# Graph attention in fp32: squares of 2 KB per partition, loads and stores two tiles at a time, six of a slot's sixteen squares on ScalarE's queue

## The chip, the cores and the metric

The kernel runs on one core of a Trainium2 chip. The metric is the device time of one execution in microseconds, lower is better. Six units matter: TensorE (PE) multiplies matrices into PSUM; VectorE (DVE), ScalarE (ACT) and GpSimd (POOL) compute on the memory; SyncE (SP) only waits, counts and issues DMAs. DMAs are issued here from two queues, SP's and ACT's, and moved by 16 DMA engines. Each unit executes its own instructions in order and waits for others by semaphores.

## The reference

For 8 graphs of 1024 nodes with 384 features, six heads of width 64:

```
q, k, v = x @ Wq + bq, x @ Wk + bk, x @ Wv + bv
scores  = q @ k^T / 8 ; masked where adj is false
probs   = softmax(scores) ; ctx = probs @ v (per head)
out     = layernorm(x + ctx @ Wf + bf)
```

`adj` is a boolean matrix of 1024 x 1024 for each graph. All is in fp32.

## The kernel before

One batch is one graph. It is worked through in 24 slots. A slot `s` stands for one tile of 128 queries and one pair of heads: `s // 6` is the group of two query tiles, `s % 6 // 2` the pair of heads, `s % 2` the query tile. Batch 0 and batch 7 are written out, batches 1 to 6 are a loop on every engine. In all there are 8 x 24 = 192 slots.

In each slot:
- PE computes the scores of two heads into PSUM (`scores`, L479), in three products of a high and a low part each. They fill the only score buffer, so the next slot's scores wait until DVE has read them.
- DVE adds the mask and takes the row's minimum while it writes SBUF (`mask_scores`, L671), once for each head.
- ACT takes the exponential in place and the row sums (`exponential`, L598).
- DVE turns each block of 32 x 32 (`turn_squares`, L684). A whole transposition of 128 x 1024 needs the blocks moved to other partitions as well.
- That is what the squares do (`move_square`, L290): sixteen DMAs within SBUF, from row block `a` (32 partitions) and column block `c` of `prob` to partition block `c` of `prob_t`. Each carries both heads, 32 partitions x 2 x 256 fp32, 64 KB. The four with `a == c` are issued by ACT (L612), the other twelve by SP (L331). Both wait until both transpositions of the slot are done, and in even slots until the context product that last read this half of `prob_t` is done.

`prob` is a ring of three slots; a slot may be written again when its squares of three slots ago have landed (L676).

For every two slots (group of slots `g`, 12 in a batch) PE makes one context product (`mix`, L499): 32 matmuls of the values with the transposed probabilities. It waits for the squares of both slots. DVE divides it by the row sums (`divide`, L695), ACT and POOL split it into a high and a low part (L606, L813). The table `STEADY` (L27 to L52) says which job stands in which slot: "m" is the context product, in slots 5, 6, 7, 9, 11 and so on to 23, and in slot 1 for the batch before; "i" spreads the inverse row sums over the partitions for it; "q", "k", "v" are projections, "x" transposes the input of the next batch, "p" is the output projection of one tile.

The order on ACT in a slot (L621) is: two exponentials, the evictions of the jobs, the squares of `move`, the high part of the context. The next slot's exponentials stand behind all of it. The order on DVE (L726) is: two masks, two transpositions, the division, then for a "p" job the addition of the residual and the moments.

SP's order in a slot (L364) is: the squares, then a load of an adjacency tile (L325, slots with `s % 6 < 2`), a load of an input tile (`X_LOADS`), a store of an output tile (`STORES`), a load of a residual tile (`RES_LOADS`). Each of these four kinds is eight DMAs a batch, one tile of 128 rows each, and each waits for a semaphore of its own; SP's next squares stand behind that wait. POOL normalises a group in the slots of `NORMALISE`, which releases the stores.

Of the kernel before, what the change touches and what calls it, by code (L numbers as in the profile page):

```python
# [14 lines left out]
P = 128  # L15
# [89 lines left out]
def graph_attention(nc, x, adj, wq, bq, wk, bk, wv, bv, wf, bf, out):  # L105
# [15 lines left out]
    with ExitStack() as ctx:  # L121
# [19 lines left out]
        prob = sb("prob", [P, 2 * RING, S], F32)  # L141
        prob_t = sb("prob_t", [P, 2, 2, 2, 4, GQ], F32)
# [25 lines left out]
        bv_wide = prob[:, 2 * RING - 1, 0:FT * P].rearrange("p (t n) -> p t n", t=FT)  # L168
# [13 lines left out]
        x_loaded = [sem(f"x_loaded{i}") for i in range(4)]  # L182
        res_loaded = [sem(f"res_loaded{g}") for g in range(4)]
        adj_loaded = [sem(f"adj_loaded{i}") for i in range(2)]
# [97 lines left out]

        def scale_rows(engine, group):
# [17 lines left out]
        @block.sync  # L301
        def _(sp):
            def load_weight(w, src):
                sp.dma_start(weight_raw[:, w], src.rearrange("(t p) n -> p t n", p=P)).then_inc(weights_in[w], 16)

            load_weight(1, wk)
            for i in range(4):
                sp.dma_start(x_in[:, i, :], x_tiles[0, :, i, :]).then_inc(x_loaded[i], 16)
            for g in (2, 3):
                sp.dma_start(res[:, 2 * g:2 * g + 2, :], x_tiles[0, :, 2 * g:2 * g + 2, :]).then_inc(res_loaded[g], 32)  # L310
            load_weight(0, wq)
            for n, bias in enumerate((bq, bk, bv)):
                sp.dma_start(bias_raw[:, n, :], bias.rearrange("(t p) -> p t", p=P),
                             allow_slow_non_contiguous=True).then_inc(biases_in, 16)
            for qt in range(2):
                sp.dma_start(adj_in[:, qt, :], adj_rows[qt * P:(qt + 1) * P, :]).then_inc(adj_loaded[qt], 16)
            load_weight(2, wv)
            load_weight(3, wf)
            sp.dma_start(bf_rows[:], bf.partition_broadcast(P)).then_inc(bf_in, 16)
            for g in range(2):  # L320
                sp.dma_start(res[:, 2 * g:2 * g + 2, :], x_tiles[0, :, 2 * g:2 * g + 2, :]).then_inc(res_loaded[g], 32)
            for i in range(RING):
                sp.sem_inc(landed[i], 256)

            def load_adjacency(b, group, qt):  # L325
                sp.wait_ge(mask_done, at(b, TT, 2 * group + qt + 1))
                sp.sem_inc(sp_waited, 1)
                row = (group + 1) * GQ + qt * P
                sp.dma_start(adj_in[:, qt, :], adj_rows[bass.ds(at(b, S, row), P), :]).then_inc(adj_loaded[qt], 16)  # L329

            def move(b, s):  # L331
                sp.wait_ge(squared, at(b, UNITS, 2 * s + 2))
                if s % 2 == 0:
                    sp.sem_inc(sp_waited, 1)
                    sp.wait_ge(mixed, at(b, GROUPS, s // 2 + 1))
                for a in range(4):
                    for c in range(4):
                        if not (a == c):
                            move_square(sp, s, a, c)

            def load_x(b, half, i):
# [6 lines left out]
                row = S + (4 * half + i) * P  # L348
                sp.dma_start(x_in[:, i, :], x_rows[bass.ds(at(b, S, row), P), :]).then_inc(x_loaded[i], 16)  # L349

            def load_residual(b, group, tile, ahead):
                sp.wait_ge(stored[group], at(b, 32, 32 * ahead))
                sp.sem_inc(sp_waited, 1)
                n = 2 * group + tile
                sp.dma_start(res[:, n, :], x_rows[bass.ds(at(b, S, ahead * S + n * P), P), :]  # L355
                             ).then_inc(res_loaded[group], 16)

            def store(b, group, tile):
                sp.wait_ge(normalised, at(b, TT, 2 * group + tile + 5))
                sp.sem_inc(sp_waited, 1)  # L360
                n = 2 * group + tile
                sp.dma_start(out_rows[bass.ds(at(b, S, n * P), P), :], res[:, n % TT, :]).then_inc(stored[group % 4], 16)  # L362

            def body(b):  # L364
                for s in range(SLOTS):
                    move(b, s)
                    if s % 6 < 2 and (s // 6 < 3 or b.mode != "last"):
                        load_adjacency(b, s // 6, s % 6)
                    if s in X_LOADS and b.mode != "last":
                        load_x(b, *X_LOADS[s])  # L370
                    if s in STORES and (STORES[s][0] >= 0 or b.mode != "first"):
                        store(b, *STORES[s])
                    if s in RES_LOADS:
                        group, tile = RES_LOADS[s]
                        if group >= 2 and b.mode != "first":
                            load_residual(b, group, tile, 0)
                        if group < 2 and b.mode != "last":
                            load_residual(b, group, tile, 1)

            body(Batch("first", 0, 0))  # L380
            with sp.Fori(0, len(loop)) as it:
                body(Batch("mid", it, 1))
            last = Batch("last", 0, BATCH - 1)
            body(last)
            for group in (2, 3):
                for tile in range(2):
                    store(last, group, tile)
            for g in range(4):
                sp.wait_ge(stored[g], 32 * BATCH)
# [3 lines left out]
        def _(pe):  # L393
# [66 lines left out]
            def run(b, job):  # L460
                bank_free(b, job)
                kind, n, piece, ahead = job
                if kind == "x":
                    if n == 0:
                        for i in range(4):
                            pe.wait_ge(x_loaded[i], at(b, 32, 16 * piece + 32) if piece == 0 else at(b, 32, 48))
# [32 lines left out]
            def mix(b, group):  # L499
# [25 lines left out]
            for n, job in enumerate(START_JOBS):  # L525
                if n == 0:
                    for i in range(4):
                        pe.wait_ge(x_loaded[i], 16)
                if n == 3:
                    for g in (2, 3):  # L530
                        pe.wait_ge(res_loaded[g], 32)
# [22 lines left out]
        def _(act):  # L554
# [42 lines left out]
            def exponential(b, t):  # L597
# [4 lines left out]
                nc.scalar.activation(prob[:, ring, :], prob[:, ring, :], ACT.Exp, scale=-1.0,  # L602
# [9 lines left out]
            def move(b, s):  # L612
# [39 lines left out]
        def _(dve):  # L652
# [18 lines left out]
            def mask_scores(b, t):  # L671
# [8 lines left out]
                nc.vector.tensor_tensor_reduce(prob[:, ring, :], score_ps[:, head, :], mask[:, s % 2, :],  # L680
# [3 lines left out]
            def turn_squares(b, t):  # L684
                ring = 2 * (t // 2 % RING) + t % 2
# [86 lines left out]
        def _(pool):  # L772
# [8 lines left out]
            def next_mask(b, group, qt):  # L781
                pool.wait_ge(adj_loaded[qt], at(b, 64, 16 * (group + 1)))
# [4 lines left out]
            def residual(b, g):  # L787
                pool.wait_ge(res_loaded[g], at(b, 32, 32))
# [77 lines left out]
            nc.gpsimd.memset(ones[:], 1.0).then_inc(ones_done, 1)  # L866
            for qt in range(2):
                pool.wait_ge(adj_loaded[qt], 16)
                make_mask(qt)
# [27 lines left out]
```

## Time and profile before

| | us |
|---|---|
| median of 3 runs (lowest, highest) | 1819.06 (1817.99, 1821.7) |
| profiled execution, its own time | 1816.15 |
| its span, first to last instruction | 1814.0 |
| PE, DVE, ACT, POOL busy | 1345.2, 1059.9, 722.3, 655.0 |
| DMA queue of SP: packets, MB | 223488, 199.07 |
| DMA queue of ACT: packets, MB | 61440, 50.38 |
| mean granted TensorE clock | 0.861 of full |

The busy times of the engines do not contain the time that an instruction queue spends on issuing a DMA. Such time stands under SPq and ACTq in the chain of waits and in the timelines. An engine whose queue issues a DMA executes nothing behind it until the issue is over. A line such as "SPq L293 DMA_DIRECT2D prob_t<-prob x12" with a start and a duration is a run of twelve issues one behind the other.

### The profile page before, as it was taken

What the parts mean: (1) busy time and instruction counts of PE and PEld (TensorE: products, weight loads), DVE (VectorE), ACT (ScalarE), POOL (GpSimd) and SP (SyncE); (2) the same over time, 40 slices, a digit from 0 to 9 for tenths busy, and PEclk for the clock granted to TensorE, in tenths of its full rate; (3) what the DMA queues carried; (4) which work ended last, traced back from release to release, by engine and by line L of the source; (5) the groups of instructions that cost most, each with busy time, mean ns of one, the idle gap of its engine ahead of it and who ended that gap; (6) DMA issues with size and microseconds to landing.
All of it is one profiled execution on the core that took longest, in us unless ns stands there. A gap on an engine that the chain in (4) does not pass through costs nothing.

```text
span 1814.0 us, 29642 instructions
## 1 busy us (share of the span) xinstructions
PE 1345.2 (74%) x8406; PEld 951.3 (52%) x8406; DVE 1059.9 (58%) x1617; ACT 722.3 (40%) x1404; POOL 655.0 (36%) x958
## 2 busy tenths in 40 slices
PE   7767796767967689676886677866888667887773
PEld 5545574545745457444574455644556445565542
DVE  5565665655656546565555655556556565566752
ACT  5443542434434434344443434434344344443330
POOL 2233541434314433154331543325433154342332
PEclk9897998878988889888898878978789788898977
DMA  5555555555555555555555555555555555555552
GB/s 154 138 136 146 144 136 141 135 151 143 128 140 140 148 139 126 142 138 149 143 128 143 139 143 141 128 140 142 146 139 132 141 146 143 144 130 149 144 137 78
DMA packets 285113, 251.62 MB, mean 139 GB/s; under 512 B 54400, under 2 KB 284928, under 8 KB 284928
## 3 DMA queue, kind: packets, MB, share of 16 engines
q1 hardware_dynamic: 223488, 199.07, 43.1%
q10 hardware_dynamic: 61440, 50.38, 11.4%
q8 instruction: 80, 1.31, 0.3%
q14 instruction: 105, 0.86, 0.2%
HBM read 35.33 MB, written 12.58 MB: 26 GB/s over the span
## 4 chain that ended last, share of the span: by engine, by line
SPq 76%; issue 10%; PE 5%; DVE 2%; ACTq 2%; ACT 2%; DMA 1%; POOL 1%; POOLq 0%; DVEq 0%
SPq L293 70%; PE context_ps L510 2%; ACTq L293 2%; DVE prob L688 2%; SPq L362 1%; SPq L329 1%; SPq L355 1%; PE score_ps L494 1%; DMA prob_t<-prob 1%; ACT prob L602 1%; SPq L349 1%; PE job_ps L399 0%; DMA x_in<-in_x_dram 0%; PE job_ps L401 0%; PE job_ps L400 0%
## 5 line engine op out<-in xcount | busy, mean ns | idle before, releaser
L510 PE MATMUL context_ps<-prob_t,v_all 128*64 128x256 f32 x3072 | 490.8, 489 | 306.5 <-DMA prob_t<-prob 306.4
L602 ACT ACTIVATE prob<-prob,row_min 128x1024 f32<-128x1024 f32 x384 | 439.6, 1146 | 530.5 <-DVE row_min L680 462.8
L680 DVE CUSTOM_DVE_ANT_0 prob<-score_ps,mask 128x1024 f32<-128x1024 f32 x384 | 454.2, 1220 | 214.0 <-PE score_ps L494 162.8
L510 PEld LDWEIGHTS context_ps<-prob_t,v_all 128*64 128x64 f32 x3072 | 301.3, 180 | 496.2 <-issue 386.7
L688 DVE STREAM_TRANSPOSE prob<-prob 128x1024 f32<-128x1024 f32 x384 | 457.9, 1231 | 151.4 <-ACT prob L602 151.4
L809 POOL TENSOR_TENSOR diag<-ident,inv_sum 128x512 f32<-128x512 f32 x96 | 99.9, 1040 | 488.4 <-DVE inv_sum L693 487.0
L610 ACT ACTIVATE context_hi<-context 128x256 fp32r<-128x256 f32 x96 | 40.1, 418 | 510.2 <-DVE context L698 385.5
L698 DVE TENSOR_TENSOR context<-context_ps,context 128x256 f32<-128x256 f32 x96 | 40.1, 418 | 317.6 <-PE context_ps L510 317.6
L803 POOL TENSOR_TENSOR q_lo<-raw,q_hi 128x256 fp32r<-128x256 f32 x95 | 69.3, 730 | 360.0 <-ACT raw L594 360.0
L399 PE MATMUL job_ps<-xt_hi,weight_hi 128*128 128x256 f32 (+1 forms) x423 | 149.4, 353 | 24.6 <-ACT raw L592 24.0
L494 PE MATMUL score_ps<-k_hi,q_hi 64*128 64x512 f32 x768 | 145.3, 457 | 20.6 <-DVE row_min L680 16.5
L401 PE MATMUL job_ps<-xt_hi,weight_lo 128*128 128x256 f32 (+1 forms) x423 | 137.1, 324 | 0.0
L400 PE MATMUL job_ps<-xt_lo,weight_hi 128*128 128x256 f32 (+1 forms) x423 | 137.0, 324 | 0.0
L494 PE MATMUL score_ps<-k_lo,q_hi 64*128 64x512 f32 x768 | 123.5, 399 | 0.0
L494 PE MATMUL score_ps<-k_hi,q_lo 64*128 64x512 f32 x768 | 122.5, 396 | 0.0
L399 PEld LDWEIGHTS job_ps<-xt_hi,weight_hi 128*128 128x128 f32 x423 | 80.9, 191 | 71.6 <-issue 36.7
L286 POOL TENSOR_SCALAR res<-res,mean_var,inv_dev 128x384 f32<-128x384 f32 x64 | 105.0, 1647 | 6.9 <-POOL inv_dev L834 6.9
L430 PE MATMUL job_ps<-diag,ones 128*64 128x256 f32 x384 | 67.8, 434 | 53.4 <-POOL diag L809 53.4
L494 PEld LDWEIGHTS score_ps<-k_hi,q_hi 64*128 64x128 f32 x768 | 59.5, 192 | 83.4 <-issue 60.8
L815 POOL TENSOR_TENSOR context_lo<-context,context_hi 128x256 fp32r<-128x256 f32 x96 | 70.5, 735 | 84.8 <-ACT context_hi L610 84.8
L803 POOL TENSOR_TENSOR k_lo<-raw,k_hi 128x512 fp32r<-128x512 f32 x46 | 58.3, 1288 | 116.1 <-ACT raw L594 116.1
L401 PEld LDWEIGHTS job_ps<-xt_hi,weight_lo 128*128 128x128 f32 x423 | 81.3, 192 | 6.7
(72 smaller groups left out, 1709.2 us busy)
## 6 DMA issues: line engine op xcount, KB each, us to landing
prob_t<-prob SPq DMA_DIRECT2D x2304, 64.0 KB, 2.0
prob_t<-prob ACTq DMA_DIRECT2D x768, 64.0 KB, 2.1
out_dram<-res SPq DMA_DIRECT2D x64, 192.0 KB, 2.1
x_in<-in_x_dram SPq DMA_DIRECT2D x60, 192.0 KB, 2.6
res<-in_x_dram SPq DMA_DIRECT2D x56, 192.0 KB
adj_in<-in_adj_dram SPq DMA_DIRECT2D x64, 128.0 KB, 2.1
res<-in_x_dram SPq DMA_DIRECT2D x4, 384.0 KB
prob_t<-in_L_gnn_Wk_dram SPq DMA_DIRECT2D x1, 576.0 KB, 3.9
```

Of the source, the lines that this page charges most:

```text
L286: engine.tensor_scalar(res[:, n, :], res[:, n, :], mean_var[:, group % 2, tile, 0:1], inv_dev[:, group % 2, tile:tile + 1], ALU.subtract, ...
L293: queue.dma_start(prob_t[32 * c:32 * c + 32, group % 2, :, qt, a, :], prob[32 * a:32 * a + 32, 2 * ring:2 * ring + 2, GQ * c:GQ * c + GQ]) ...
L399: pe.matmul(dst, left_hi, right_hi, start=(t == 0), stop=False)
L400: pe.matmul(dst, left_hi, right_lo, start=False, stop=False)
L401: last = pe.matmul(dst, left_lo, right_hi, start=False, stop=(t == FT - 1))
L494: last[head] = pe.matmul(score_ps[:, head, keys], q_part[rows, pair, q], k_part[rows, pair, keys], start=(n == 0), stop=(n == 2))
L510: last = pe.matmul(context_ps[64 * head:64 * head + 64, 0:GQ], v_all[:, kt, col:col + HS], keys, start=(kt == 0), stop=(kt == TT - 1))
L602: nc.scalar.activation(prob[:, ring, :], prob[:, ring, :], ACT.Exp, scale=-1.0, bias=row_min[:, ring:ring + 1], accum_out=row_sum[:, s // ...
L680: nc.vector.tensor_tensor_reduce(prob[:, ring, :], score_ps[:, head, :], mask[:, s % 2, :], 1.0, HUGE, ALU.add, ALU.min, row_min[:, ring:r ...
L688: nc.vector.transpose(prob[:, ring, :], prob[:, ring, :]).then_inc(squared, 1)
L803: nc.gpsimd.tensor_tensor(lo, copy[:, 0:width], hi, ALU.subtract).then_inc(lo_done, 1)
L809: nc.gpsimd.tensor_tensor(diag[:], ident[:].unsqueeze(1).to_broadcast([P, 4, P]), inv_sum[:, group % 2, :].unsqueeze(2).to_broadcast([P, 4 ...
```

## The change

`prob` gets the form [ring of 3][4 column blocks][2 heads][256] and `prob_t` has the two heads behind the row block, so that a square is one run of 512 fp32 (2 KB) per partition on both sides, where it was two runs of 1 KB. The mask, the exponential and the transposition of one head now work on four pieces of 256 with gaps of 256 between them, and the context product reads its keys with another step.

The squares with `(a + c) % 3 == 0` are ACT's: six of sixteen. SP keeps ten.

Input, residual, adjacency and output tiles are moved two at a time: 16 DMAs a batch instead of 32. The semaphores count accordingly, and each such DMA waits for the later of its two tiles.

```diff
-STORES = {5: (-2, 0), 6: (-2, 1), 12: (-1, 0), 13: (-1, 1), 15: (0, 0), 16: (0, 1), 19: (1, 0), 20: (1, 1)}
-RES_LOADS = {8: (2, 0), 9: (2, 1), 14: (3, 0), 15: (3, 1), 18: (0, 0), 19: (0, 1), 22: (1, 0), 23: (1, 1)}
-X_LOADS = {1: (0, 0), 2: (0, 1), 3: (0, 2), 4: (0, 3), 11: (1, 0), 12: (1, 1), 13: (1, 2), 14: (1, 3)}
+STORES = {5: -2, 12: -1, 16: 0, 20: 1}
+RES_LOADS = {8: 2, 15: 3, 19: 0, 23: 1}
+X_LOADS = {2: (0, 0), 4: (0, 1), 11: (1, 0), 14: (1, 1)}
...
-        prob = sb("prob", [P, 2 * RING, S], F32)
-        prob_t = sb("prob_t", [P, 2, 2, 2, 4, GQ], F32)
+        prob = sb("prob", [P, RING, 4, 2, GQ], F32)
+        prob_t = sb("prob_t", [P, 2, 2, 4, 2, GQ], F32)
...
+        def probabilities(t):
+            return prob[:, t // 2 % RING, :, t % 2, :]
...
-            queue.dma_start(prob_t[32 * c:32 * c + 32, group % 2, :, qt, a, :],
-                            prob[32 * a:32 * a + 32, 2 * ring:2 * ring + 2, GQ * c:GQ * c + GQ]
+            queue.dma_start(prob_t[32 * c:32 * c + 32, group % 2, qt, a].rearrange("p h n -> p (h n)"),
+                            prob[32 * a:32 * a + 32, ring, c].rearrange("p h n -> p (h n)")
                             ).then_inc(landed[ring], 16)
...
-                        if not (a == c):
+                        if not ((a + c) % 3 == 0):
                             move_square(sp, s, a, c)
...
-            def store(b, group, tile):
-                sp.wait_ge(normalised, at(b, TT, 2 * group + tile + 5))
+            def store(b, group):
+                sp.wait_ge(normalised, at(b, TT, 2 * group + 6))
...
-                        keys = prob_t[:, group % 2, head, :, :, 32 * kt:32 * kt + 32].rearrange(
+                        keys = prob_t[:, group % 2, :, :, head, 32 * kt:32 * kt + 32].rearrange(
                             "p q a j -> p (q a) j")
...
-                        if a == c:
+                        if (a + c) % 3 == 0:
                             move_square(act, s, a, c)
...
-                nc.vector.tensor_tensor_reduce(prob[:, ring, :], score_ps[:, head, :], mask[:, s % 2, :],
+                nc.vector.tensor_tensor_reduce(probabilities(t), in_quarters(score_ps[:, head, :]),
+                                               in_quarters(mask[:, s % 2, :]),
...
-                nc.vector.transpose(prob[:, ring, :], prob[:, ring, :]).then_inc(squared, 1)
+                nc.vector.transpose(probabilities(t), probabilities(t)).then_inc(squared, 1)
```

`in_quarters` looks at 1024 columns as four times 256.

## Rows read from the trace of the kernel before

**Rows 1.** The page: busy time, share and instructions of each engine.

```profile
PE 1345.2 (74%) x8406; PEld 951.3 (52%) x8406; DVE 1059.9 (58%) x1617; ACT 722.3 (40%) x1404; POOL 655.0 (36%) x958
```

**Rows 2.** The page: the chain that ended last, shares by engine's queue or engine.

```profile
SPq 76%; issue 10%; PE 5%; DVE 2%; ACTq 2%; ACT 2%; DMA 1%; POOL 1%; POOLq 0%; DVEq 0%
```

**Rows 3.** SP's queue in order of time: start, us, what.

```profile
307.98 8.47 SPq L293 DMA_DIRECT2D prob_t<-prob  x12
...
812.14 7.67 SPq L293 DMA_DIRECT2D prob_t<-prob  x12
820.14 0.35 SPq L329 DMA_DIRECT2D adj_in<-in_adj_dram  x1
820.76 0.34 SPq L349 DMA_DIRECT2D x_in<-in_x_dram  x1
```

**Rows 4.** Line 293, the squares' issues on both queues.

```profile
L293 SPq DMA_DIRECT2D prob_t<-prob x2304: 585/597/1980, 32.3 to 1788.7; - x192
L293 ACTq DMA_DIRECT2D prob_t<-prob x768: 592/619/2363, 33.5 to 1780.7; - x192
DMA to landing us min/median/max: 2.0/2.0/4.4
```

**Rows 5.** SP's queue in order of time, first issue of batches 2 and 3.

```profile
468.83 0.63 SPq L293 DMA_DIRECT2D prob_t<-prob  x1
...
692.82 1.26 SPq L293 DMA_DIRECT2D prob_t<-prob  x2
```

**Rows 6.** PE in order of time, two context products.

```profile
65.13 3.62 PE L510 MATMUL context_ps<-prob_t,v_all 128*64 128x256 f32 x32
...
801.79 6.30 PE L510 MATMUL context_ps<-prob_t,v_all 128*64 128x256 f32 x32 [4.47 <-DMA prob_t<-prob]
```

**Rows 7.** ACT in order of time, batch 0 and, last, slot 18 of batch 3.

```profile
54.14 2.55 ACTq L293 DMA_DIRECT2D prob_t<-prob  x4
56.74 1.15 ACT L602 ACTIVATE prob<-prob,row_min 128x1024 f32<-128x1024 f32 x1 [2.89 <-DVE row_min L680]
...
68.86 2.76 ACTq L293 DMA_DIRECT2D prob_t<-prob  x4
...
85.02 2.54 ACTq L293 DMA_DIRECT2D prob_t<-prob  x4
...
105.12 3.27 ACTq L293 DMA_DIRECT2D prob_t<-prob  x4
...
855.11 2.54 ACTq L293 DMA_DIRECT2D prob_t<-prob  x4
```

**Rows 8.** DVE in order of time.

```profile
51.73 2.38 DVE L688 STREAM_TRANSPOSE prob<-prob 128x1024 f32<-128x1024 f32 x2 [1.78 <-ACT prob L602]
...
58.13 2.38 DVE L688 STREAM_TRANSPOSE prob<-prob 128x1024 f32<-128x1024 f32 x2 [1.70 <-ACT prob L602]
...
79.84 2.37 DVE L688 STREAM_TRANSPOSE prob<-prob 128x1024 f32<-128x1024 f32 x2 [1.74 <-ACT prob L602]
...
833.18 0.52 DVE L705 TENSOR_TENSOR res<-job_ps,res 128x384 f32<-128x384 f32 x1
...
836.59 1.22 DVE L680 CUSTOM_DVE_ANT_0 prob<-score_ps,mask 128x1024 f32<-128x1024 f32 x1
...
850.95 2.39 DVE L688 STREAM_TRANSPOSE prob<-prob 128x1024 f32<-128x1024 f32 x2 [0.28 <-ACT prob L602]
```

**Rows 9.** Groups of instructions by shape: busy us, mean ns, idle before.

```profile
L610 ACT ACTIVATE context_hi<-context 128x256 fp32r<-128x256 f32 x96 | 40.1, 418 | 510.2 <-DVE context L698 385.5 <-issue 124.7
...
L583 ACT ACTIVATE xt_hi<-job_ps 128x512 fp32r<-128x512 f32 x42 | 25.4, 604 | 0.0
L592 ACT ACTIVATE raw<-job_ps 128x512 f32<-128x512 f32 x42 | 25.3, 602 | 0.0
```

**Rows 10.** SP's queue in order of time, at the start of the program.

```profile
1.26 1.90 SPq L308 DMA_DIRECT2D x_in<-in_x_dram  x4
3.20 0.97 SPq L310 DMA_DIRECT2D res<-in_x_dram  x2
```

More of the change, by code:

```diff
@@ L181, in graph_attention @@
         ones_done = sem("ones_done")
-        x_loaded = [sem(f"x_loaded{i}") for i in range(4)]
+        x_loaded = [sem(f"x_loaded{i}") for i in range(2)]
         res_loaded = [sem(f"res_loaded{g}") for g in range(4)]
-        adj_loaded = [sem(f"adj_loaded{i}") for i in range(2)]
+        adj_loaded = sem("adj_loaded")
         mask_done = sem("mask_done")
@@ L281, in job_parts, with in_quarters @@
             return GQ, q_hi[:, pair, :], q_lo[:, pair, :]
+        def probabilities(t):
+            return prob[:, t // 2 % RING, :, t % 2, :]
+        def in_quarters(keys):
+            return keys.rearrange("p (c n) -> p c n", c=4)
         def scale_rows(engine, group):
@@ L306, in _ @@
             load_weight(1, wk)
-            for i in range(4):
-                sp.dma_start(x_in[:, i, :], x_tiles[0, :, i, :]).then_inc(x_loaded[i], 16)
+            for i in range(2):
+                sp.dma_start(x_in[:, 2 * i:2 * i + 2, :], x_tiles[0, :, 2 * i:2 * i + 2, :]).then_inc(x_loaded[i], 16)
             for g in (2, 3):
-                sp.dma_start(res[:, 2 * g:2 * g + 2, :], x_tiles[0, :, 2 * g:2 * g + 2, :]).then_inc(res_loaded[g], 32)
+                sp.dma_start(res[:, 2 * g:2 * g + 2, :], x_tiles[0, :, 2 * g:2 * g + 2, :]).then_inc(res_loaded[g], 16)
             load_weight(0, wq)
@@ L320, in _, with load_adjacency @@
             for g in range(2):
-                sp.dma_start(res[:, 2 * g:2 * g + 2, :], x_tiles[0, :, 2 * g:2 * g + 2, :]).then_inc(res_loaded[g], 32)
+                sp.dma_start(res[:, 2 * g:2 * g + 2, :], x_tiles[0, :, 2 * g:2 * g + 2, :]).then_inc(res_loaded[g], 16)
             for i in range(RING):
                 sp.sem_inc(landed[i], 256)
-            def load_adjacency(b, group, qt):
-                sp.wait_ge(mask_done, at(b, TT, 2 * group + qt + 1))
+            def load_adjacency(b, group):
+                sp.wait_ge(mask_done, at(b, TT, 2 * group + 2))
                 sp.sem_inc(sp_waited, 1)
-                row = (group + 1) * GQ + qt * P
-                sp.dma_start(adj_in[:, qt, :], adj_rows[bass.ds(at(b, S, row), P), :]).then_inc(adj_loaded[qt], 16)
+                sp.dma_start(adj_in[:], adj_rows[bass.ds(at(b, S, (group + 1) * GQ), GQ), :].rearrange(
+                    "(q p) k -> p q k", p=P)).then_inc(adj_loaded, 16)
             def move(b, s):
@@ L347, in load_x, with load_residual @@
                     sp.sem_inc(sp_waited, 1)
[L348 to L352, printed above, removed]
-                sp.sem_inc(sp_waited, 1)
-                n = 2 * group + tile
-                sp.dma_start(res[:, n, :], x_rows[bass.ds(at(b, S, ahead * S + n * P), P), :]
-                             ).then_inc(res_loaded[group], 16)
-            def store(b, group, tile):
-                sp.wait_ge(normalised, at(b, TT, 2 * group + tile + 5))
+                row = S + (4 * half + 2 * i) * P
+                sp.dma_start(x_in[:, 2 * i:2 * i + 2, :], x_rows[bass.ds(at(b, S, row), GQ), :].rearrange(
+                    "(t p) h -> p t h", p=P)).then_inc(x_loaded[i], 16)
+            def load_residual(b, group, ahead):
+                sp.wait_ge(stored[group], at(b, 16, 16 * ahead))
+                sp.sem_inc(sp_waited, 1)
+                n = 2 * group
+                sp.dma_start(res[:, n:n + 2, :], x_rows[bass.ds(at(b, S, ahead * S + n * P), GQ), :].rearrange(
+                    "(t p) h -> p t h", p=P)).then_inc(res_loaded[group], 16)
+            def store(b, group):
+                sp.wait_ge(normalised, at(b, TT, 2 * group + 6))
                 sp.sem_inc(sp_waited, 1)
-                n = 2 * group + tile
-                sp.dma_start(out_rows[bass.ds(at(b, S, n * P), P), :], res[:, n % TT, :]).then_inc(stored[group % 4], 16)
+                n = 2 * group
+                sp.dma_start(out_rows[bass.ds(at(b, S, n * P), GQ), :].rearrange("(t p) h -> p t h", p=P),
+                             res[:, n % TT:n % TT + 2, :]).then_inc(stored[group % 4], 16)
             def body(b):
@@ L366, in body @@
                     move(b, s)
-                    if s % 6 < 2 and (s // 6 < 3 or b.mode != "last"):
-                        load_adjacency(b, s // 6, s % 6)
+                    if s % 6 == 1 and (s // 6 < 3 or b.mode != "last"):
+                        load_adjacency(b, s // 6)
                     if s in X_LOADS and b.mode != "last":
                         load_x(b, *X_LOADS[s])
-                    if s in STORES and (STORES[s][0] >= 0 or b.mode != "first"):
-                        store(b, *STORES[s])
+                    if s in STORES and (STORES[s] >= 0 or b.mode != "first"):
+                        store(b, STORES[s])
                     if s in RES_LOADS:
-                        group, tile = RES_LOADS[s]
+                        group = RES_LOADS[s]
                         if group >= 2 and b.mode != "first":
-                            load_residual(b, group, tile, 0)
+                            load_residual(b, group, 0)
                         if group < 2 and b.mode != "last":
-                            load_residual(b, group, tile, 1)
+                            load_residual(b, group, 1)
             body(Batch("first", 0, 0))
@@ L385, in _ @@
             for group in (2, 3):
-                for tile in range(2):
-                    store(last, group, tile)
+                store(last, group)
             for g in range(4):
-                sp.wait_ge(stored[g], 32 * BATCH)
+                sp.wait_ge(stored[g], 16 * BATCH)
         @block.tensor
@@ L464, in run @@
                     if n == 0:
-                        for i in range(4):
-                            pe.wait_ge(x_loaded[i], at(b, 32, 16 * piece + 32) if piece == 0 else at(b, 32, 48))
+                        for i in range(2):
+                            pe.wait_ge(x_loaded[i], at(b, 32, 16 * piece + 32))
                     transpose_x(b.mode, job)
@@ L526, in _ @@
                 if n == 0:
-                    for i in range(4):
+                    for i in range(2):
                         pe.wait_ge(x_loaded[i], 16)
@@ L530, in _ @@
                     for g in (2, 3):
-                        pe.wait_ge(res_loaded[g], 32)
+                        pe.wait_ge(res_loaded[g], 16)
                 if n >= 4:
@@ L601, in exponential @@
                 act.wait_ge(masked, at(b, UNITS, t + 3))
-                nc.scalar.activation(prob[:, ring, :], prob[:, ring, :], ACT.Exp, scale=-1.0,
+                nc.scalar.activation(probabilities(t), probabilities(t), ACT.Exp, scale=-1.0,
                                      bias=row_min[:, ring:ring + 1],
@@ L781, in next_mask @@
             def next_mask(b, group, qt):
-                pool.wait_ge(adj_loaded[qt], at(b, 64, 16 * (group + 1)))
+                pool.wait_ge(adj_loaded, at(b, 64, 16 * (group + 2)))
                 pool.wait_ge(masked, at(b, UNITS, 12 * group + 2 * qt))
@@ L787, in residual @@
             def residual(b, g):
-                pool.wait_ge(res_loaded[g], at(b, 32, 32))
+                pool.wait_ge(res_loaded[g], at(b, 16, 16))
                 if g >= 2 and b.mode == "first":
@@ L866, in _ @@
             nc.gpsimd.memset(ones[:], 1.0).then_inc(ones_done, 1)
+            pool.wait_ge(adj_loaded, 32)
             for qt in range(2):
-                pool.wait_ge(adj_loaded[qt], 16)
                 make_mask(qt)
```

5 lines of the change are left out of this document (2 added, 3 removed).

## The prediction

> **What bounds the kernel now.** I read the page first. The span is 1814.0 us and no compute engine is full: PE 74%, DVE 58%, ACT 40% [rows 1]. The chain of waits says where the time is: 76% of it lies on SP's issuing queue, 5% on PE, 2% each on DVE and ACT's queue [rows 2]. So I read SP's queue in order of time. Twelve squares take 7.67 us, 0.64 each from start to start, and behind them comes a load at once [rows 3]. Each issue holds its queue for a median 597 ns on SP and 619 ns on ACT, and the data are there 2.0 us after the issue [rows 4]. One middle batch, from its first issue to that of the next, takes 692.8 - 468.8 = 224.0 us [rows 5], 9.33 per slot. SP's own work in that is 288 x 0.64 = 184, 32 loads and stores at about 0.61 (820.14 to 820.76 is one, with its register work) = 20, and some 11 for squares that take 1 us and more (8.47 us for a slot's twelve at 307.98, where 7.67 is the usual): 215 of 224. SP is the bound, with a small rest for places where it has to wait.
>
> What waits in turn is PE: the context product needs the squares landed, so PE starts it late, at 801.79 only after 4.47 us of idling [rows 6].
>
> **What the change takes off SP.** Two of twelve squares a slot: 48 x 0.64 = 31 us a batch. Half of the loads and stores: 16 x 0.61 = 10. SP's work falls to about 240 x 0.64 + 16 x 0.61 + 2 + 8 = 174 a batch, 7.2 per slot. If SP alone set the pace, that were 1814 - 8 x 41 = 1486 us. It does not, because the work removed turns up on ACT's queue, and there it lies in a loop.
>
> **The loop through ACT.** ACT issues its squares when both transposes of the slot are done, and its next exponential stands behind them. In a slot with nothing else late: four issues 2.55 us (the set at 54.14), exponential 1.15, then 0.24 to the transposes, 2.38 for both. The transposes end at 51.73 + 2.38 = 54.11 and at 58.13 + 2.38 = 60.51: 6.40 us per slot [rows 7, 8]. This loop is hidden now behind SP's 9.33. With six issues it is 6.40 + 2 x 0.645 = 7.69. Per middle batch:
> - 24 plain slots: 24 x 7.69 = 184.6.
> - The high part of the context stands behind the issues in twelve slots and moves the next exponential by up to its 0.42 [rows 9]: 5.0.
> - Slots 10 and 18 evict three x jobs: ACT's issues begin at 855.11, 1.77 after the transposes end (850.95 + 2.39) [rows 7, 8]; slot 10 I take at 2.3. Together 4.0.
> - Slot 4's move waits for the first context product: ACT's issues come at 68.86 instead of 60.51, 8.35 late; slot 6's at 85.02 instead of 79.84 + 2.37 = 82.21, 2.8 late [rows 7, 8]. The second wait is for work that was released earlier, so 1.3 of it is used up by the longer issuing: 8.3 + 1.5 = 9.8.
> - After a slot with two p jobs DVE is late, not ACT: from 833.18 to the next mask at 836.59 are 3.4 us, then mask 1.28, exponential 1.15, 0.24, 2.38 = 8.45 [rows 8]. That is 0.8 over the plain slot, in two slots: 1.6.
> - Issues that overlap with SP's are longer: a set of four at 3.27 beside the usual 2.55 [rows 7]. I take 0.14 per slot, an estimate a fifth of the way to that set, 3.4.
>
> Sum 208.4, against 224.0 now: 15.6 saved in each of six middle batches, 94. The first batch starts without a backlog on SP and its slots already run by this loop; the last has few evictions and is paced half by it; for both I count no gain. At the very end ACT's last issue begins at 1780.7 and SP's at 1788.7 [rows 4]; ACT's set of four began 3 x 0.65 earlier, at 1778.7, with the transposes' end, and nine steps of 0.64 from there are 1784.5: 4 more. Then 1814 - 98 = 1716 span; the profiled execution took 1816.15 us for a span of 1814.0, and the median of the runs is 1819, so 1718 to 1721. I take 1718.
>
> **What has to fit beside it.** SP needs 7.2 per slot of 8.7, so it drops off the path, and squares land about 6.8 + 2.0 = 8.8 us after their transposes; the product that needs them comes two slots on, 17 us, and has to be over by about 1.3 us after the transposes of its slot so as not to hold the next slot: scores and first mask take some 3 us more, and ACT is ready for them after its 3.9 of issues and 0.4. PE's busy time is 1345 / 192 = 7.0 per slot [rows 1] and would fit; a product right behind other work took 3.62 us instead of 6.30 after a wait [rows 6], so PE gets lighter when it waits less. In slots 5, 6 and 7 a product stands in each, and there the cover is thin; that is the 9.8 above.
>
> **The merged loads and stores.** They wait for the later of two tiles, in slots where that tile is long done: the normalisation of group 1 is in slot 18 and its store in 20. They are worth nothing beyond the 10 us on SP. Behind the wait of a store stand SP's next squares; a wait of a slot there would be 8 us a batch, and would show only where it exceeds SP's 1.5 us of slack per slot.
>
> **The new layout.** Probabilities are now written by DVE and ACT in four runs of 256 with gaps. The nearest rows: ACT writes 128x512 in such a broken pattern in 604 ns and in a flat one in 602 [rows 9]. So nothing, taken as 0. DVE has no such pair in this trace; the other end is 5% on the mask, the exponential and both transposes (4.75 us a slot on the loop), 0.24 per slot, +46 us. Below zero there is no reason.
>
> **The price of one issue** is what decides. A square was [2 runs x 32 partitions] of 1 KB and is now one run of 2 KB. Does the queue charge for runs? At the program's start four loads of one run took 1.90 us, 0.475 each, and two loads of two runs 0.97, 0.485 each [rows 10]: a second run cost nothing there. So I take a square at its present 0.64, which is the row nearest to it: SBUF to SBUF, 32 partitions. The other end is the loads' 0.475, should two broken patterns at once be what makes squares dear. Dearer than now there is no reason for in the shape.
>
> The trace shows 0.64 us of SP's queue per square, twelve in a row, as the bound [rows 3]. Against this stands the Trainium skill, "DMA: Bandwidth & Descriptors", section "Issuing engines are not separate DMA queues", which says that issuing from several engines only saves the sequencer's time, "which is usually small relative to the DMA itself". Here the trace disagrees with "usually small". By the rule the change would be worth about nothing, 1816 us, which is the third rival.
>
> **Rivals.**
> 1. A square gets cheaper to issue, 0.475. For: loads of any number of runs cost that. Against: those same rows show that runs are not what costs. The loop becomes 7.69 - 6 x 0.17 = 6.67; on 21 slots (the others are led by DVE or a product) 21 less per batch: 187, PE's 24 x 7.0 = 168 still below. Six batches at 37, the outer two at about 20 each, the end 4: 1816 - 266 = 1550 us.
> 2. Slower: ACT's queue. Both queues are released by the same transposes, while now SP is some slots' work behind. If every issue on ACT goes at the pace of the worst set, 3.27 / 4 = 0.82 instead of 0.645 [rows 7], a slot gains 6 x 0.175 = 1.05 and a batch 24 to 25: 233, so 1816 + 9 x 6 = 1870. It decides from 15.6 / 144 = 0.11 per issue, a price of 0.75. For: such sets exist. Against: SP issues almost without a break now too, so the overlap is already in the usual 2.55.
> 3. No gain: the moved issues only change queue, and the landing of squares, not SP's pace, holds PE: 1816. Against: landing stays at 2.0 while SP's queue is behind.
>
> **How the numbers follow.** The forecast has 0.63, with its own range 1665 to 1760 (the layout's 46 above; an issue cheaper by 0.04 below, 21 x 6 x 0.04 x 7 = 35, and slots 4 to 7 either way). The cheaper issue has 0.25, slower 0.08, no gain 0.04. The range reaches from 1515 to 1760. This kernel's runs can tell 0.2% (3.6 us) from no change; faster by more than that 0.88, within it 0.04, slower 0.08.
>
> **What would show it.** Right: the chain of waits leaves SP and runs through ACT's issues, exponentials and transposes; SP has waits on the transposes in nearly every slot; ACT's sets of six last 3.9 us; a middle batch takes about 208; transposes and mask keep 1.23 and 1.22. Wrong: squares issued in 0.5 or less (rival 1); sets of six of 4.6 and more (rival 2); a transposition above 1.25; PE idling before its context products as it does now.

## The result and the profile after

The changed kernel takes 1763.62 us (median of 4 runs, 1760.43 to 1773.09), beside 1818.53 us for the kernel before (4 runs, 1816.36 to 1821.7): ratio 0.9705, 95% interval 0.9664 to 0.9747. It is faster by 55 us. The forecast was 1718, its range ended at 1760. The profiled execution took 1761.29 us with a span of 1759.2, at a mean granted TensorE clock of 0.878 (before 0.861).

The page: busy times, and the chain that ended last by engine and by line. They answer to [rows 1, 2].

```profile
PE 1316.1 (75%) x8406; PEld 943.4 (54%) x8406; DVE 1041.8 (59%) x1617; ACT 711.8 (40%) x1404; POOL 656.5 (37%) x958
...
ACTq 36%; issue 20%; DVE 19%; ACT 12%; PE 9%; POOL 2%; DVEq 1%; DMA 0%; SPq 0%; POOLq 0%
ACTq L301 34%; DVE prob L697 16%; ACT prob L611 7%; PE context_ps L519 4%; ACT raw L603 1%; ACT k_hi L596 1%; PE score_ps L503 1%; DVE stats L721 1%; DVE res L714 1%; PE job_ps L408 1%; PE job_ps L409 1%; PE job_ps L410 1%; ACT xt_hi L592 1%; PE job_ps L439 1%; ACT raw L601 1%
```

SP's queue has gone from 76% of the chain to 0, and the loop has come in its place: ACT's issues of squares (L301), the exponential (L611), the transpositions (L697). The groups of the page, busy us and mean ns, then idle before and its releaser, say that no instruction got dearer through the new layout:

```profile
L697 DVE STREAM_TRANSPOSE prob<-prob 128x1024 f32<-128x1024 f32 x384 | 456.6, 1227 | 520.9 <-ACT prob L611 520.9
L611 ACT ACTIVATE prob<-prob,row_min 128x1024 f32<-128x1024 f32 x384 | 437.1, 1139 | 499.6 <-issue 294.9
L689 DVE CUSTOM_DVE_ANT_0 prob<-score_ps,mask 128x1024 f32<-128x1024 f32 x384 | 451.8, 1213 | 102.1 <-PE score_ps L503 82.1
L519 PE MATMUL context_ps<-prob_t,v_all 128*64 128x256 f32 x3072 | 423.1, 437 | 59.3 <-DMA prob_t<-prob 59.1
```

The same group of context products before, from its page. PE's wait for squares was five times as long, and its matmuls took 489 ns on average, where they take 437 now. The granted clock makes that difference: at the lower level (1.2 GHz) such a matmul takes 637 ns on average before and 635 after, at the higher (2.4 GHz) 380 and 379. Before, 1172 of the 3072 ran wholly at the lower level, after the change 596. The two products that the prediction compared differ in the same way: over the one of 3.62 us the granted clock was 1.00, over the one of 6.30 us 0.57.

```profile
L510 PE MATMUL context_ps<-prob_t,v_all 128*64 128x256 f32 x3072 | 490.8, 489 | 306.5 <-DMA prob_t<-prob 306.4
```

What SP waits for now, us in total, times, longest: the transpositions, in most slots.

```profile
SPq L342 <- DVE prob L697: 122.5, 84, 19.6
SPq L301 <- DVE prob L697: 107.4, 77, 4.9
SPq L301 <- PE context_ps L519: 68.2, 15, 9.4
```

The issues of squares, which answer to [rows 4]; the numbers after x1920 and x1152 are min/median/max ns:

```profile
L301 SPq DMA_DIRECT2D prob_t<-prob x1920: 507/591/2246, 31.9 to 1731.5; - x192
L301 ACTq DMA_DIRECT2D prob_t<-prob x1152: 514/614/2090, 33.1 to 1729.3; - x192
```

The medians are 591 and 614 ns after 597 and 619. Only the minimum fell, 585 to 507. It belongs to the first square of a set: its median went from 605 to 508 ns on SP and from 593 to 522 on ACT. The others are hardly cheaper, and from start to start they still lie 0.63 apart.

How long a middle batch is, I read from the first transpositions of batches 1 and 7, DVE in order of time:

```profile
238.27 2.37 DVE L697 STREAM_TRANSPOSE prob<-prob 128x1024 f32<-128x1024 f32 x2 [4.13 <-ACT prob L611]
...
1530.05 2.37 DVE L697 STREAM_TRANSPOSE prob<-prob 128x1024 f32<-128x1024 f32 x2 [3.19 <-ACT prob L611]
```

(1530.05 - 238.27) / 6 = 215.3 us. Before, the same two stand at 237.05 and 1578.11: 223.5. So six middle batches gave 49 us, where 94 had been forecast. Batch 1 starts 1.2 later, and from batch 7's first transpositions to the span's end there are 6.8 us less (229.1 after 235.9), where 4 had been forecast. The length of a middle batch is worked out in this way in all that follows.

Now the sets of six, ACT's and SP's queues in order of time in slots 14, 15, 16 and (835.11) 18 of a middle batch:

```profile
800.81 3.73 ACTq L301 DMA_DIRECT2D prob_t<-prob  x6
804.66 1.15 ACT L611 ACTIVATE prob<-prob,row_min 128x1024 f32<-128x1024 f32 x1 [4.55 <-issue]
...
808.46 4.07 ACTq L301 DMA_DIRECT2D prob_t<-prob  x6
...
816.81 3.74 ACTq L301 DMA_DIRECT2D prob_t<-prob  x6
...
835.11 5.47 ACTq L301 DMA_DIRECT2D prob_t<-prob  x6
```

```profile
800.93 6.46 SPq L301 DMA_DIRECT2D prob_t<-prob  x10
...
808.45 7.00 SPq L301 DMA_DIRECT2D prob_t<-prob  x10
...
816.93 6.46 SPq L301 DMA_DIRECT2D prob_t<-prob  x10
```

Where SP starts 0.12 us after ACT (800.93, 816.93) the set takes 3.73, where both start together (808.45) 4.07. Over all 192 slots ACT's second issue has a median of 867 ns in the 94 slots in which SP starts between 0.5 before and 0.05 after ACT, instead of 614; in the 63 in which SP starts 0.05 to 0.3 later, SP's second has 769 instead of 591. A set takes 4.12 on average.

A few sets are far longer (5.47 at 835.11), because one issue in them is. Of ACT's 1152 issues 28 take over 1.1 us. Beside 27 of these 28 a DMA packet starts that isn't the kernel's own, but of the kind that the page of the profile calls "instruction" (between 0.5 us before the issue and its end); so it does beside only 97 of the other 1124. On SP it is 58 of 60 issues, and 151 of the other 1860. So the long issues go with the loading of program code. That the loading is their cause is my reading of this coincidence; no run changed it by itself.

### The profile page after: what moved, and what is told of

Its sections match the earlier page's. It is cut to its first block, busy times and chain, and to the rows that moved or that the text cites. A ratio compares the mean times of both kernels' runs of the same rounds, so it can differ in the third digit from the quotient of the medians.

```text
span 1759.2 us, 29185 instructions
## 1 busy us (share of the span) xinstructions
PE 1316.1 (75%) x8406; PEld 943.4 (54%) x8406; DVE 1041.8 (59%) x1617; ACT 711.8 (40%) x1404; POOL 656.5 (37%) x958
## 4 chain that ended last, share of the span: by engine, by line
ACTq 36%; issue 20%; DVE 19%; ACT 12%; PE 9%; POOL 2%; DVEq 1%; DMA 0%; SPq 0%; POOLq 0%
ACTq L301 34%; DVE prob L697 16%; ACT prob L611 7%; PE context_ps L519 4%; ACT raw L603 1%; ACT k_hi L596 1%; PE score_ps L503 1%; DVE stats L721 1%; DVE res L714 1%; PE job_ps L408 1%; PE job_ps L409 1%; PE job_ps L410 1%; ACT xt_hi L592 1%; PE job_ps L439 1%; ACT raw L601 1%
## 5 line engine op out<-in xcount | busy, mean ns | idle before, releaser
L697 DVE STREAM_TRANSPOSE prob<-prob 128x1024 f32<-128x1024 f32 x384 | 456.6, 1227 | 520.9 <-ACT prob L611 520.9
L611 ACT ACTIVATE prob<-prob,row_min 128x1024 f32<-128x1024 f32 x384 | 437.1, 1139 | 499.6 <-issue 294.9
L689 DVE CUSTOM_DVE_ANT_0 prob<-score_ps,mask 128x1024 f32<-128x1024 f32 x384 | 451.8, 1213 | 102.1 <-PE score_ps L503 82.1
L519 PE MATMUL context_ps<-prob_t,v_all 128*64 128x256 f32 x3072 | 423.1, 437 | 59.3 <-DMA prob_t<-prob 59.1
L519 PEld LDWEIGHTS context_ps<-prob_t,v_all 128*64 128x64 f32 x3072 | 266.3, 161 | 216.6 <-issue 134.0
L408 PE MATMUL job_ps<-xt_hi,weight_hi 128*128 128x256 f32 (+1 forms) x423 | 153.2, 362 | 94.5 <-ACT raw L601 51.8
L503 PE MATMUL score_ps<-k_hi,q_hi 64*128 64x512 f32 x768 | 150.0, 470 | 66.4 <-DVE row_min L689 49.8
L439 PE MATMUL job_ps<-diag,ones 128*64 128x256 f32 x384 | 80.3, 504 | 115.5 <-POOL diag L818 65.9
L410 PE MATMUL job_ps<-xt_hi,weight_lo 128*128 128x256 f32 (+1 forms) x423 | 141.2, 334 | 0.0
L409 PE MATMUL job_ps<-xt_lo,weight_hi 128*128 128x256 f32 (+1 forms) x423 | 140.9, 333 | 0.0
L503 PE MATMUL score_ps<-k_lo,q_hi 64*128 64x512 f32 x768 | 128.3, 413 | 0.0
L503 PE MATMUL score_ps<-k_hi,q_lo 64*128 64x512 f32 x768 | 127.2, 409 | 0.0
L439 PEld LDWEIGHTS job_ps<-diag,ones 128*64 128x64 f32 x384 | 22.5, 160 | 151.1 <-issue 94.4
L408 PE MATMUL job_ps<-weight_hi,xt_hi 128*128 128x384 f32 x192 | 70.7, 368 | 42.1 <-ACT raw L603 26.7
```

The source lines that it names most:

```text
L408: pe.matmul(dst, left_hi, right_hi, start=(t == 0), stop=False)
L409: pe.matmul(dst, left_hi, right_lo, start=False, stop=False)
L410: last = pe.matmul(dst, left_lo, right_hi, start=False, stop=(t == FT - 1))
L439: last = pe.matmul(job_bank(b.mode, job)[64 * head:64 * head + 64, 0:GQ], ones[:], diag[:, 2 * head:2 * head + 2, :], start=True, stop=True)
L503: last[head] = pe.matmul(score_ps[:, head, keys], q_part[rows, pair, q], k_part[rows, pair, keys], start=(n == 0), stop=(n == 2))
L519: last = pe.matmul(context_ps[64 * head:64 * head + 64, 0:GQ], v_all[:, kt, col:col + HS], keys, start=(kt == 0), stop=(kt == TT - 1))
```

## The experiments

Each gives its ratio to the kernel before on the same chip; that took 1811.45 us beside the split undone, the split alone, SP's squares behind ACT's and the changed kernel written out; 1814.61 beside the kernel before written out, five squares and nothing else, and five squares written out; 1810.07 beside the others.

**The split undone.** The changed kernel with layout and merged loads, but four squares on ACT.

```diff
-                        if (a + c) % 3 == 0:
+                        if a == c:
```

> The changed kernel with the split of before (ACT 4 squares, SP 12), so layout and merged loads alone. Theory (the change moved the bound from SP's queue into the loop transposes - ACT's issues - exponential): ACT's sets are back at 2.6 us, the loop at 6.4, and SP is the bound again, with 12 x 0.634 and half the loads: 10 us a batch less than before, so about 1819 - 80 = 1740 us, faster than the changed kernel. Rival A (the six-ten split brings the whole gain, loads were hidden): 1810 to 1820. Rival B (layout slows DVE or PE): above 1820, with transposes over 1.25 us.

1723.59 us, ratio 0.9504 (0.9467 to 0.954), a middle batch 211.05. That is 16 us below the 1740 expected. By the ratios the change is 2.0%, some 37 us, faster without its split than with it. SP bounds again:

```profile
SPq 79%; issue 9%; PE 7%; ACT 2%; DMA 1%; DVE 1%; ACTq 1%; POOL 0%; POOLq 0%; DVEq 0%
```

**The split alone.** The kernel before with `(a + c) % 3 == 0` in place of `a == c`.

> The kernel before with the six-ten split alone: old layout, 32 loads and stores a batch. Theory: SP's work is 240 x 0.64 + 20 + 10 = 184 us a batch, under the loop's 215, so the loads are hidden and the time is that of the changed kernel, 1760 to 1775; the first issue of a set costs 0.59 and not 0.52 (+0.07 x 191 = 13 us more). Rival (SP is still the bound in the changed kernel and merged loads bring the gain): 1800 and more.

1764.28 us, ratio 0.9738 (0.9708 to 0.9768): the whole change has 0.9705, and the intervals overlap. Once ACT's loop is the bound, layout and merged loads show nothing beyond the noise.

**Merged loads alone**, on the old layout and the old split.

> The kernel before with merged loads and stores alone; old layout, four squares on ACT. Against it stands the run with merged loads and the new layout, 1723.6. Theory (SP is the bound, so each issue that goes counts fully): 16 x 0.61 = 10 us a batch off 223.5, and the layout brings only the cheaper first square of a set (0.59 to 0.51) and 0.006 per square, 3 to 4 us a batch: so 1735 to 1750 here. Rival (the new layout brings half or more of the gain): 1765 to 1790.

1753.97 us, ratio 0.9687 (0.9656 to 0.9718), 4 us above the range expected; a middle batch came as expected. It went from 223.5 to 213.8: SP's time between its sets of squares fell from 28.9 to 19.5 a batch, the 9.4 that the 16 DMAs cost. The step from here to the split undone is the layout: 2.8 us a middle batch where 3 to 4 were expected, 30 us between the medians and 23.6 between the spans (1746.8, 1723.2). SP's mean issue is 621 ns with it and 630 without, over 2304 of them 22 us: the layout's gain is in SP's issues.

**SP's squares behind ACT's**, so that the two sets don't start together.

```diff
             def move(b, s):
                 sp.wait_ge(squared, at(b, UNITS, 2 * s + 2))
+                sp.sem_inc(sp_waited, 1)
+                sp.wait_ge(act_issued, at(b, SLOTS, s + 1))
...
                             move_square(act, s, a, c)
+                act.sem_inc(act_issued, 1)
```

> The changed kernel, SP's ten squares wait until ACT has issued its six. In the changed kernel ACT's second issue takes 867 ns where both queues start together (94 slots) and 614 where SP starts later. Theory (collision of the queues lengthens the loop): ACT's sets fall from 4.12 to about 3.75 us, 0.37 x 192 = 71 us less on the loop, against which squares land 3.9 us later; where products then wait (slots 5 to 7 above all) some 20 us come back: about 1715. Rival (the sets are long for another cause, such as fetching instructions): sets stay at 4.0 and more, and the time is 1765 to 1800 because squares come later.

1765.37 us, ratio 0.9728 (0.9691 to 0.9765): no gain. The collision did go: ACT's second issue has a median of 618 ns. But its sets average 3.95 us and not 3.75, and 21 of its issues still take over 1.1 us, all 21 beside a packet of the kind "instruction". ACT in order of time:

```profile
692.83 3.74 ACTq L302 DMA_DIRECT2D prob_t<-prob  x6
700.55 3.74 ACTq L302 DMA_DIRECT2D prob_t<-prob  x6
```

But SP's squares now end later, the chain has them and the products instead, and a middle batch stays at 215.5:

```profile
ACTq 26%; issue 19%; PE 18%; DVE 14%; ACT 9%; SPq 8%; DMA 3%; POOL 2%; DVEq 1%; POOLq 0%
```

**Batches 1 to 6 written out** instead of looped, on all five engines, in the changed kernel.

```diff
-            with act.Fori(0, len(loop)) as it:
+            for it in range(len(loop)):
```

> The changed kernel with the six middle batches written out instead of a loop; same work. In the changed kernel slot 23 to slot 0 takes 11.5 us against 8.2 in other slots of its kind, and both ACT (2.69) and DVE (2.91) idle there behind nothing that the profile shows. Theory (the loop's edge costs each engine some 2.5 us, formerly hidden behind SP): that step falls to about 8.5 and the time by 6 x 2.7 = 16 us, to 1748. Rival (it is the k jobs or instruction fetch of any kind): unchanged at 1764 or slower, with long issues all over.

1733.65 us, ratio 0.9562 (0.953 to 0.9594), a middle batch 210.9. By the ratios that is 26 us where 16 were expected. The step from slot 23 to the next batch took 11.5 on average and takes 8.35. The changed kernel, ACT at one such edge in order of time:

```profile
658.47 5.36 ACTq L301 DMA_DIRECT2D prob_t<-prob  x6
663.94 0.42 ACT L619 ACTIVATE context_hi<-context 128x256 fp32r<-128x256 f32 x1 [5.89 <-issue]
667.04 1.15 ACT L611 ACTIVATE prob<-prob,row_min 128x1024 f32<-128x1024 f32 x1 [2.69 <-issue]
```

The same place, written out:

```profile
654.76 4.01 ACTq L301 DMA_DIRECT2D prob_t<-prob  x6
658.83 0.42 ACT L619 ACTIVATE context_hi<-context 128x256 fp32r<-128x256 f32 x1 [4.49 <-issue]
659.15 1.14 ACT L611 ACTIVATE prob<-prob,row_min 128x1024 f32<-128x1024 f32 x1
```

From the start of the context's high part to that of the exponential there are 3.10 us across the loop's edge and 0.32 without it, and 2.69 of it has no releaser but the engine's own "issue". The other four turns of the loop have 2.98 to 3.04, the step out of the loop 0.32. In each of the five turns a packet of the kind "instruction" starts 1.2 to 1.3 us after the high part, and a second one between 1.8 us before and 0.5 us after it; at the step out of the loop, and at these places in the written-out kernel, there is none. The edge shown, from 663.94 to 667.04 (packets, MB, share of the 16 DMA engines):

```profile
q8 instruction: 1, 0.02, 2.0%
q14 instruction: 1, 0.01, 0.9%
```

Written out, long issues are left, 28 on ACT as before, but at other places.

**The kernel before, written out.**

> The kernel before, with batches 1 to 6 written out. Theory: SP works behind the transpositions and the other engines' edges hide in its backlog, but SP has an edge of its own between its last issue of one batch and its first of the next, 0.5 to 3 us: 1790 to 1808 against 1811 to 1818. Rival: the edge is hidden wholly, within 0.3% of the kernel before.

1766.9 us, ratio 0.9744 (0.9721 to 0.9768), 23 us below the lowest time expected. The edge of the loop on SP's queue in the kernel before, and then written out:

```profile
688.72 0.45 SPq L355 DMA_DIRECT2D res<-in_x_dram  x1
692.82 7.66 SPq L293 DMA_DIRECT2D prob_t<-prob  x12
```

```profile
674.20 0.52 SPq L355 DMA_DIRECT2D res<-in_x_dram  x1
674.84 8.10 SPq L293 DMA_DIRECT2D prob_t<-prob  x12
```

SP stands still for 692.82 - 689.17 = 3.65 us, against 0.12; over the five turns it is 3.2 to 3.65, always against 0.12. Over a middle batch 28.9 us between the sets become 21.5. Of these 7.4 us 2.8 are at the edge (six batches share five turns), the rest is spread over the other slots with loads and stores. The batch takes 214.9 instead of 223.5. Nothing but the loop is gone, and the kernel before gains 2.6%, nearly as much as the whole change with its 3.0%.

**Five squares on ACT** in the changed kernel, eleven on SP.

```diff
-                        if (a + c) % 3 == 0:
+                        if a == c or (a, c) == (0, 3):
```

> The changed kernel with five squares on ACT and eleven on SP. Two bounds are now measured: with six on ACT the loop through ACT makes 215.3 us a middle batch, with four SP makes 211.1. Theory (each is linear in the issues): the loop gives 215.3 - 24 x 0.65 = 199.7, SP gives 211.1 - 24 x 0.63 = 195.9; the larger plus some 2 for their meeting: about 202 a batch, 1764 - 8 x 13.5 = 1655 us (1640 to 1680). Rival (the two do not trade, something common such as PE or the products' landing holds at 210): 1715 to 1725.

1652.18 us, ratio 0.9119 (0.9089 to 0.9149), as expected; a middle batch 201.1, ACT's sets 3.30. The chain is shared:

```profile
SPq 33%; issue 19%; PE 14%; ACTq 11%; DVE 10%; ACT 6%; POOL 4%; DMA 2%; DVEq 0%; POOLq 0%
```

One square per slot put back is worth 5.9% by the ratios, some 106 us.

**Five squares on ACT and nothing else**, in the kernel before.

> The kernel before with one edit: the square (0, 3) is ACT's too, five of sixteen; old layout, loads and stores one tile at a time. Theory: SP is the bound with 11 squares a slot and twice the loads: merged loads and layout were worth 11 us a batch at four squares on ACT, so here 1652 plus some 60 to 85: 1720 (1700 to 1740). Rival: at five the ACT loop already hides layout and loads, as it does at six: 1650 to 1670.

1715.9 us, ratio 0.9465 (0.9443 to 0.9487), as expected. So with five on ACT layout and merged loads are worth 64 us by the medians (1652.18), with four 88 (1723.59 beside 1811.45), with six nothing that shows.

**ACT's squares of a slot behind the exponentials of the next**, with six and with five squares.

```diff
                         exponential(b, 2 * s + 1)
+                    if s or b.mode != "first":
+                        move(b, s - 1)
...
-                    if s < SLOTS:
-                        move(b, s)
```

> The changed kernel, still six squares on ACT, but ACT issues those of slot s behind both exponentials of slot s + 1. Theory (it is the loop transposes - issues - exponential that holds the changed kernel, not ACT's sum of work): a slot costs ACT 4.1 issues + 2.3 exponentials + 1.4 evictions + 0.2 = 8.0 us instead of 8.97, and the wait of 8.3 in slot 4 loses most of its weight: 185 to 195 a batch, 1580 to 1640 us. Rival (ACT's issues are a bound by their sum, or squares that come later hold the products): 1700 and more.

> As the run before, with five squares on ACT and eleven on SP. Theory: ACT's sum is 7.35 per slot, SP's 264 x 0.633 + 10 + 9 = 186 a batch, 7.75 per slot, so SP is the bound again with its coupling of 1.05 (211 against 201 of own work with twelve): 195 a batch, 1590 to 1640 us, within 20 of the run before. Rival (PE at 7.0 per slot and the products in slots 5 to 7 hold both): both above 1660.

1706.59 us with six (ratio 0.9423, 0.9373 to 0.9472), 1652.76 with five (0.9123, 0.9093 to 0.9153); both miss. With six the new order still gains some 51 us on the changed kernel by the ratios: the exponentials no longer wait behind issues. But the evictions do. Waits with six, in us in total, times, longest; "issue" stands here for ACT's own issuing of squares:

```profile
ACT context L586 <- issue: 203.6, 64, 4.5
ACT q_hi L596 <- issue: 178.6, 70, 4.2
```

```profile
DVE context L707 <- ACT context L586: 143.6, 60, 4.0
```

```profile
PE context_ps L519 <- DMA prob_t<-prob: 97.1, 35, 5.6
```

The context waits for its eviction, and the product for squares issued a part of a slot later. With five the new order changes nothing (1652.76 beside 1652.18): the chain is 41% SP's queue and 23% PE.

**Five squares on ACT, written out.**

> The whole change with five of sixteen squares on ACT, and batches 1 to 6 written out instead of looped on every engine. Theory: two bounds stand side by side (SP's issuing and the loop through ACT), and the edge of the loop holds both, about 3 to 5 us per batch: 1625 (1615 to 1640) against 1652 with the loop. Rival: the edge costs only where ACT's loop is the bound, and SP catches up over it: 1645 to 1655.

1642.53 us, ratio 0.9052 (0.9037 to 0.9067), the fastest version; yet only 12 us better than looped by the ratios, between the two expectations. The time from SP's last square of a batch to its next set fell from 4.36 to 0.81, and part of it came back as a wait for the context product, first SP with the loop, then written out:

```profile
SPq L301 <- PE context_ps L519: 15.9, 11, 4.6
```

```profile
SPq L301 <- PE context_ps L519: 51.8, 15, 6.8
```

## Why the prediction was right in its mechanism and wrong in its size

**SP as the bound before, and off the path after**: right. The chain left SP's queue entirely, and the first experiment brings it back by the split alone. But my account of SP's 224 us was short of a term: I had put the 9 us that were left over down to "places where it has to wait". Written out, SP's time between sets is 7.4 us a batch shorter: 2.8 at the edge of SP's loop, 4.6 in the other slots. So most of the rest was the price of the loop.

**The loop through ACT**: right in its parts. Plain slots take 7.65 to 7.9 us (forecast 7.69), most slots with the context's high part before the exponential 8.1 to 8.5 (forecast 7.69 + 0.42 = 8.11), ACT's lag in slot 4 is 8.3 us, slot 6 is 0.5 shorter than forecast. The slot table of the forecast was the right tool.

**The step that failed is the sum per middle batch, 208.4; it is 215.3.** These 6.9 us times six are 41 of the 43 us between 1716 and 1759.2. (The outer batches nearly cancel: batch 1 starts 1.2 later, the end gives 2.8 more than forecast; and a middle batch before took 223.5 by the transpositions, not 224.0.) They come apart so:
- The edge of the loop, 3.2 a batch, was no term at all; it was put at nothing without a word. It was hidden before: DVE, ACT and PE arrived there with SP behind them, and SP had its own. I took the loop's price from slots in the middle of a batch, and a loop that has become the bound pays at its edge too: five turns take 12.2 from slot 23 to slot 0, and the step out of the loop, into batch 7, takes 8.2. Part of it is the set of slot 23, 5.05 on average and 4.20 written out. Written out, the batch is 4.4 shorter, 3.2 of it at this one place.
- Issues beside SP's: I took a set at 3.87 + 0.14 = 4.01. In middle batches the other 23 sets take 94.5 us, and 23 x 4.01 = 92.2: 2.3 more. The common start of the two queues was not mis-sized: the 119 of these 138 sets without an issue over 1.1 us average 3.97. What makes the excess is the 19 long issues in the other sets, together 3.3 us a batch above the usual 0.614; 18 of them stand in slots 7, 10, 12 and 18. With SP held back there are still 15 sets above 4.6 us in the whole run, where there were 26, so they don't come from the common start alone. All but one of the 28 long issues of the run stand beside a packet of the kind "instruction", which was no term of the sum either.
- The remaining 1.4 I can't assign.

Holding SP back took the common start away and gave no time back: its squares came later instead, and the chain had them and the products.

**Layout**: its cost of nothing is right (transposition 1227 ns after 1231, mask 1213 after 1220). That an edit on SP could still bring 24 to 30 us without the split was outside the sum, rightly: beside six squares on ACT it brings none.

**Merged loads**: 9.4 us a batch on SP, forecast 10; worth 56 us alone and none with the split. The sentence of the Trainium skill, weighed in the prediction, that the time to initiate a DMA is usually small relative to the DMA itself ("DMA: Bandwidth & Descriptors", section "Issuing engines are not separate DMA queues") does not hold for these squares: an issue holds its queue for 0.6 us, and the data are there 2.0 us after it. One issue a slot moved to the other queue, and nothing else, gave 5.35%, some 97 us.

**Rivals.** A cheaper issue (1550) is false: only the first of a set fell, by 0.07 to 0.10. The slower ACT queue (1870) exists with sets of 4.12 instead of 3.87, 0.04 per issue and not 0.175, and the kernel is faster. No gain is false. The price of an issue, which I had called what decides, was right at 0.64. It had stretched the range down by 200 us, while upwards stood only 40, for the layout; no bound of it was for a term that the sum lacked.

**What the prediction did not ask** is whether six was the right number. Its own figures had it: SP's 7.2 per slot beside a loop of 8.7, so the bound had been moved past the balance by more than one square's 0.64; with five they would stand at 7.9 and 8.0. Measured, a slot then takes 201.1 / 24 = 8.4, and the kernel 1652 us.

## What to carry over

When work is moved from the queue that bounds to one that lies in a loop of waits, write down both paces for each split and take the one where they meet; here one square of sixteen is worth some 100 us, more than everything else in the change. When the bound moves to another engine, its loop edge, and every cost that the old bound covered, becomes a term of the sum: look for the gap before the first instruction of each turn of the loop on each engine, and for packets of the kind "instruction" beside long issues. An edit that only relieves an engine shows nothing in the state in which another engine bounds, so test the parts of a change alone before calling one worthless.

## What the runs showed of the hardware

- The turn of the loop stops an engine for some 3 us: 2.7 to 2.8 between the same two instructions on ACT (2.98 to 3.10 against 0.32), 3.1 to 3.5 on SP's queue (3.2 to 3.65 against 0.12). On ACT, packets of the kind "instruction" start there in each of the five turns, and none does where the loop is written out.
- Nearly every issue that takes over 1.1 us instead of 0.6 has such a packet beside it: 27 of 28 on ACT and 58 of 60 on SP in the changed kernel, against 8 to 9% of the others.
- A square of one 2 KB run per partition is issued in a median of 508 ns on SP and 522 on ACT when it is the first of a set, against 605 and 593 with two runs of 1 KB; in a row both take some 0.63 to 0.64 from start to start.
- When SP and ACT begin issuing within 0.05 us of each other, ACT pays about 0.25 us once, on its second issue (867 instead of 614 ns). Where SP starts 0.12 us later, ACT's set stays at 3.73, and it is SP's second issue that is dearer (769 instead of 591 ns).
